# A decoder layer on one core: causal masks of the maxima as 64+64 columns, 25 warm-up transposes, one drain on GpSimd

## The reference

```python
x = layernorm(x + attn(x))          # causal self-attention, 16 heads of 16 channels, with biases
x = layernorm(x + xattn(x, ctx))    # cross-attention to 64 context rows, mask on the query side
x = layernorm(x + ffn(x))           # ternary weights, activations rounded to 8 bits, silu(gate) * up

att = einsum('bhqd,bhkd->bhqk', q, k) * 0.25
att = where(tril, att, -inf)        # the causal mask
y   = einsum('bhqk,bhkd->bhqd', softmax(att), v)
```

## Time and profile before

| | |
|---|---|
| time, median of 3 runs | 889.46 us (888.61 to 890.96) |
| profiled execution | 889.83 us, its span 888.1 us |
| TensorE busy | 818.7 us (92%) |
| VectorE busy | 676.0 us (76%) |
| ScalarE busy | 581.7 us (65%) |
| GpSimd busy | 388.2 us (44%) |
| L961, scores of the maxima | 119.0 us in 768 matmuls |
| L965, mask of 128 columns | 53.5 us in 512 matmuls |
| L968, mask of 64 columns | 48.4 us in 512 matmuls |

### The profile page before, as it was taken

One profiled execution on the slowest core, in us unless ns is written; L12 is line 12 of the kernel. 1 busy time (PEld: TensorE's weight loads), 2 busy tenths in 40 slices (PEclk: granted clock), 3 DMA queues, 4 the chain that ended last, 5 costly groups with the idle time before them and its releaser, 6 DMA issues.

```text
span 888.1 us, 21732 instructions
## 1 busy us (share of the span) xinstructions
PE 818.7 (92%) x8199; PEld 383.3 (43%) x8225; DVE 676.0 (76%) x1179; ACT 581.7 (65%) x759; POOL 388.2 (44%) x621
## 2 busy tenths in 40 slices
PE   7788889899999999999999999999999999998875
PEld 4433334343554434534454344543535443445533
DVE  6888798558877698877997589774898857835588
ACT  3177765367874588565775669666597469864485
POOL 6533284545343345533434634462524413452244
PEclk9999999999999999999999999999999999999999
DMA  7543123210420111120331112120220000010001
GB/s 207 172 119 82 38 63 94 73 37 19 114 73 2 37 36 39 43 84 2 73 85 49 34 28 49 44 69 16 54 58 25 26 2 1 2 49 1 2 1 49
DMA packets 47814, 45.50 MB, mean 51 GB/s; under 512 B 9698, under 2 KB 43874, under 8 KB 47714
## 3 DMA queue, kind: packets, MB, share of 16 engines
q1 hardware_dynamic: 43698, 39.12, 16.1%
q0 software_dynamic: 1536, 3.15, 1.5%
q10 hardware_dynamic: 2480, 1.84, 0.8%
HBM read 14.55 MB, written 4.19 MB: 21 GB/s over the span
## 4 chain that ended last, share of the span: by engine, by line
PE 77%; DVE 11%; ACT 7%; issue 3%; DMA 1%; POOL 1%; SPq 0%; POOLq 0%; DVEq 0%; ACTq 0%
PE ps L1002 15%; PE ps L987 14%; PE ps L799 10%; PE ps L961 7%; PE ps L814 6%; DVE shift L1316 5%; PE ps L933 4%; PE ps L860 3%; ACT probs L1105 3%; PE ps L945 2%; PE ps L788 2%; DVE shift_h L1316 2%; PE ps L890 2%; PE ps L871 2%; PE ps L885 2%
## 5 line engine op out<-in xcount | busy, mean ns | idle before, releaser
L1105 ACT ACTIVATE probs<-ps 128x1024 f32<-128x1024 f32 (+3 forms) x384 | 297.5, 810 | 148.8 <-PE ps L987 146.0
L1316 DVE TENSOR_REDUCE shift<-ps 128x2 f32<-128x1024 f32 (+2 forms) x224 | 249.8, 1145 | 53.4 <-PE ps L961 28.1
L987 PE MATMUL ps<-q_stack,k_stack 64*128 64x512 bf16 (+3 forms) x1536 | 179.5, 325 | 12.5 <-DVE shift L1316 3.8
L688 POOL TENSOR_SCALAR_AFFINE_SELECT probs<-probs 128x512 f32<-128x512 f32 x128 | 81.1, 639 | 193.2 <-ACT probs L1105 192.6
L1002 PE MATMUL ps<-probs,v_aug 128*32 128x512 f32 (+3 forms) x1536 | 158.8, 497 | 0.7 <-POOL probs L688 0.6
L961 PE MATMUL ps<-k_stack,q_stack 64*128 64x512 bf16 (+3 forms) x768 | 119.0, 327 | 15.6 <-ACT probs L1105 5.6
L1316 DVE TENSOR_REDUCE shift_h<-ps 128x4 bf16<-128x512 f32 (+2 forms) x96 | 98.0, 1046 | 18.6 <-PE ps L968 18.2
L987 PEld LDWEIGHTS ps<-q_stack,k_stack 64*128 64x128 bf16 x1536 | 54.0, 94 | 116.5 <-ACT probs L1105 37.2
L961 PEld LDWEIGHTS ps<-k_stack,q_stack 64*128 64x128 bf16 x768 | 39.7, 93 | 115.5 <-ACT probs L1105 38.9
L1229 DVE TENSOR_REDUCE shift<-ps 128x8 bf16<-128x512 f32 x64 | 40.6, 685 | 26.5 <-PE ps L871 26.4
L1002 PEld LDWEIGHTS ps<-probs,v_aug 128*32 128x32 f32 x1536 | 33.6, 108 | 48.8 <-issue 37.4
(11 more groups left out here) (186 smaller groups left out, 1391.7 us busy)
## 6 DMA issues: line engine op xcount, KB each, us to landing
q_stack<-part_sb SPq DMA_DIRECT2D x168, 64.0 KB, 2.0
k_stack<-part_sb SPq DMA_DIRECT2D x144, 64.0 KB, 2.0
xT<-in_x_cols SPq DMA_DIRECT2D x8, 512.0 KB, 4.9
xt<-in_x SPq DMA_DIRECT2D x8, 512.0 KB, 3.9
out_x<-xt SPq DMA_DIRECT2D x7, 512.0 KB, 3.0
k_stack<-part_sb POOLq DMA_DIRECT2D x48, 64.0 KB, 2.3
q_stack<-shiftT SPq DMA_DIRECT2D x128, 1.0 KB
q_stack<-part_sb ACTq DMA_DIRECT2D x24, 64.0 KB, 2.7
```

The source lines that it names most:

```text
L688: pool.affine_select(out=blk, in_=blk, compare_op=ALU.is_ge, fill=0.0, base=0, pattern=[[0, HG], [1, P]], channel_multiplier=-1).then_inc( ...
L987: mm = pe.matmul(ps[:, u.banks[i], 0:BANK - off], k_stack[rows, part, h, kb * P:(kb + 1) * P], q_stack[rows, part, c, h, off:BANK], start= ...
L1105: act.activation(probs_of(b, n)[:, 2 * p:2 * p + 2, :], pair(u)[:, :, 0:BANK - off], ACT.Exp).then_inc(probs_ready, 1)
L1316: dve.tensor_reduce(to[:, :, pairs[0]:pairs[-1] + 1, qb % TH], pair(u)[:, :, 0:len(pairs) * w].rearrange("p j (h w) -> p j h w", w=w), AX. ...
```

## The change

`pick_h` grows from 192 to 256 columns, and what it and `causal` hold changes: the second half of `causal`'s columns now has the mask of the second 64 keys, and `pick_h[rows, 0:128]` and `pick_h[rows, 128:256]` are the weights for the first and the second 64 keys. For this GpSimd runs six selections per row half instead of two. `max_unit` adds the mask in two parts of 64 columns each. The number of mask matmuls and their place in the order stay. TensorE's transposes at the start go from 15 to 25, and GpSimd executes a drain after `make_masks`.

```diff
--- before.py
+++ after.py
@@ -330,7 +330,7 @@
         ident, ident_h = sb("ident", [P, P]), sb("ident_h", [P, P], BF16)
         ones, ones_h = sb("ones", [P, P]), sb("ones_h", [P, P], BF16)
 
-        pick_h, causal = sb("pick_h", [P, P + HALF], BF16), sb("causal", [P, P], BF16)
+        pick_h, causal = sb("pick_h", [P, 2 * P], BF16), sb("causal", [P, P], BF16)
 
         maskT = sb("maskT", [TK + H, T], BF16)
         off_pick = sb("off_pick", [TK + H, H, TK], BF16)
@@ -621,10 +621,18 @@
             made(pool.memset(pick_h[:], 0.0))
             made(pool.memset(causal[:], 0.0))
             for rows in four:
-                made(pool.affine_select(out=pick_h[rows], in_=pick_h[rows], compare_op=ALU.not_equal, fill=1.0, base=HALF,
-                                        pattern=[[-1, P + HALF]], channel_multiplier=1))
+                made(pool.affine_select(out=pick_h[rows], in_=pick_h[rows], compare_op=ALU.not_equal, fill=1.0, base=0,
+                                        pattern=[[-1, 2 * P]], channel_multiplier=1))
+                made(pool.affine_select(out=pick_h[rows], in_=pick_h[rows], compare_op=ALU.not_equal, fill=1.0, base=P + HALF,
+                                        pattern=[[-1, 2 * P]], channel_multiplier=1))
+                made(pool.affine_select(out=pick_h[rows, P + HALF:2 * P], in_=pick_h[rows, P + HALF:2 * P], compare_op=ALU.not_equal,
+                                        fill=0.0, base=1 - HALF, pattern=[[0, HALF]], channel_multiplier=1))
+                made(pool.affine_select(out=pick_h[rows, P:P + HALF], in_=pick_h[rows, P:P + HALF], compare_op=ALU.not_equal,
+                                        fill=1.0, base=1 - HALF, pattern=[[0, HALF]], channel_multiplier=1))
                 made(pool.affine_select(out=causal[rows], in_=causal[rows], compare_op=ALU.is_ge, fill=NEG, base=0,
-                                        pattern=[[-1, P]], channel_multiplier=1))
+                                        pattern=[[0, 2], [-1, HALF]], channel_multiplier=1))
+                made(pool.affine_select(out=causal[rows, HALF:P], in_=causal[rows, HALF:P], compare_op=ALU.not_equal, fill=NEG,
+                                        base=1 - HALF, pattern=[[0, HALF]], channel_multiplier=1))
             made(pool.memset(shift_h[:], 0.0))
             made(pool.memset(q_stack[:, 1, :, :, :].rearrange("p c h q -> p (c h q)").bitcast(F32), 0.0))
             pool.memset(v2[:], 1.0).then_inc(consts_ready, 1)
@@ -677,6 +685,7 @@
                         move_piece(pool, g, n, first_main, first_rest)
                     if (g, h) == (1, 1):
                         make_masks()
+                        pool.drain()
                 if u.kind == "tern":
                     n = u.idx
                     pool.wait_ge(tern_ready, n + 1)
@@ -806,7 +815,7 @@
                 if kind == "kq":
                     t, e, h = pieces[u.idx]
                     if b == 0 and u.idx == 0:
-                        stir(u, 15)
+                        stir(u, 25)
                     if b == 0 and u.idx < 2:
                         pe.wait_ge(kq_loaded[1 - t], 16)
                     pe.wait_ge(x_loaded[h], 16 * (b + 1))
@@ -961,12 +970,11 @@
                         mm = pe.matmul(ps[:, u.banks[s], end - w:end], q_stack[rows, 0, c, h, qb % TH * P:(qb % TH + 1) * P],
                                        k_stack[rows, 0, h, k0:k0 + w], start=True, stop=not diag)
                     if diag:
-                        for s, rows in enumerate(four):
-                            pe.matmul(ps[:, u.banks[s], end - P:end], pick_h[rows, HALF:P + HALF], causal[rows, :],
-                                      start=False, stop=False)
-                        for s, rows in enumerate(four):
-                            mm = pe.matmul(ps[:, u.banks[s], end - HALF:end], pick_h[rows, 0:P], causal[rows, 0:HALF],
-                                           start=False, stop=True)
+                        for part in range(2):
+                            at, keys = slice(part * P, (part + 1) * P), slice(part * HALF, (part + 1) * HALF)
+                            for s, rows in enumerate(four):
+                                mm = pe.matmul(ps[:, u.banks[s], end - P + part * HALF:end - HALF + part * HALF], pick_h[rows, at],
+                                               causal[rows, keys], start=False, stop=part == 1)
                 mm.then_inc(max_scores, 1)
 
             def scores(u):
```

## The result

| | before | after |
|---|---|---|
| median | 889.55 us (4 runs) | 879.95 us (879.04 to 880.97, 4 runs) |
| ratio | | 0.9891, 95% interval [0.9874, 0.9908] |
| profiled execution | 889.83 us, span 888.1 | 879.04 us, span 877.3 |

The kernel got 9.6 us faster, not 5.4. The time lies under the range of the forecast, and the two parts that the forecast counted (4.5 for the masks, 1.2 for the warm-up) cannot fill the gap. Further on, a time beside a ratio is a median, and the gain or loss beside it is worked out from the ratio where nothing else is said.

What follows compares the result with a forecast made beforehand. TensorE was taken as the bound, with 77% of the chain of waits and 96% busy in the middle. 889.83 - 4.5 (masks) - 1.2 (warm-up) = 884.1 us, mask building and drain 0; 8-in-10 range 881.5 to 888.8.

Steps and rivals of the forecast that it cites:

- Masks, -4.5 us: Diagonal-block mask matmuls on TensorE, first pair 64 wide instead of 128: 4.5 us less, ends 3.0 and 7.7.
- The pitch of 0.03 us for narrow pairs: TensorE's 64-column mask pairs pass in 0.03 us, against 0.06 for wide ones, saving 0.030 us a pair.
- The rule on weight loads: TensorE's mask matmuls: about 81 ns a matmul at 128 columns, set by loads too, so narrowing gives 0.
- Building the masks, 0: GpSimd's longer set-up at the start, 3.6 us covered by idle time: 0, ends 0 and +1.0 us.
- Warm-up, -1.2 us: 25 transposes on TensorE at the start raise the clock earlier: two thirds of 1.76 us, 1.2 us less.
- The rule that transposes do not count for the clock: TensorE's start: transposes do not count as busy for the clock, so the warm-up costs its whole 1.1 us.
- case 3: Start on TensorE: warm-up buys nothing and delays by 1.1 us, masks still gain 4.5; 886.4 us, chance 0.13.
- The drain, 0 with ends 0 and +0.2 us: Added GpSimd drain after the masks are built ends inside a 7 us wait for ScalarE: costs 0 to 0.2 us.
- rival 4: TensorE's clock falls more often as mask work thins, 1.65 us a fall; five falls give 893.6 us, chance 0.09.

Runs made afterwards that it cites:

- the doubled masks: The kernel before with every mask pair of 128 columns given twice: 899.17 us, 1.0101 [1.0083, 1.0119].

## Why the prediction was wrong

- **Masks, -4.5 us: right.** Alone they gave 4.6, with an interval of 3.3 to 5.9. The pitch of 0.03 us for narrow pairs held. The split of it was a little off: I took 4/5 of the 5.6 us on the chain; what holds is 0.6 of all 7.7 us.
- **The rule on weight loads** that the forecast set aside (the Trainium skill, "TensorE: Matmul & The Clock Gate", "Back-to-back issue gap") would have made this part 0; the measured 4.6 us settles it for these pairs of half-height matmuls.
- **Building the masks, 0: right.** GpSimd's constants are ready at 13.0, expected at 13.2. GpSimd's own first move comes 0.7 us late for it (expected 0.3), and the chain to the first maximum does not wait for that move.
- **Warm-up, -1.2 us: right.** -1.2 alone, 1.5 on top of the rest, both small beside their intervals; the traces show it better, where ScalarE's first copy starts 1.55 and 1.66 us earlier than with 15 transposes, 1.2 us earlier than with one. The 25 transposes span 5.16 and 4.73 us, under the 5.8 of the low rate, and the first projection behind them runs at 2.4 GHz; so the engine had run only transposes before the clock rose. The rule that transposes do not count for the clock (the Trainium skill, same page, "Part 4: PE-mode transpose") made case 3; the runs contradict it.
- **The drain, 0 with ends 0 and +0.2 us: this step failed.** It brought 4.5 us alone and 3.3 on top of the other two parts. I priced the added drain where it stands (it is indeed covered, 2.03 us in 7 us of idle time) and never asked what it takes off later work. The kernel has 18 drains of its own, and the trace of before showed the one that mattered: GpSimd idle for 5.83 us "<-issue" before L708, TensorE for 3.53 us "<-issue" before L871, and 2.88 us of "issue" on the chain. I read that the chain had 3% of "issue" and did not look where. In these kernels a drain pays 0.084 us for every software DMA since the last drain; the early one takes over 24 of the 48, so the one on the chain is 2.0 us shorter.
- **The clock, as rival 4: right kind, wrong sign.** I asked whether thinner work would add stretches at 1.2 GHz. The wait of 3.5 us for the drain came with such a stretch in the profiles of the kernel before, of the masks alone, of the warm-up alone, of both together and of the doubled masks, and in no profile with a shorter drain; filling the wait gave 2.0 us back by the ratio, 1.5 at its place in the profiled pair. So 2.0 us are drain and about 1.5 clock, which makes the 3.3 to 3.6 us that the first qcast brings in the profiled pairs. The 1 us or so by which the ratio of the drain alone lies above that is not explained; its interval begins at 3.5 us. Where the other stretches of low clock fall differs from profile to profile, and what steers them stays open. The forecast missed the median by 4.2 us, which the 3.3 to 4.5 of this step cover. The profiled pair is 10.8 us apart, and the differences at 802 us (1.6 us gained) and at 132 us (1.1 us lost), where one of the two has a fall of the clock and the other has not, are tied to no part of the change by any run.

## What to carry to other kernels

Search the trace for idle time "<-issue" on the chain of waits and look up which instruction of the sequencer fills it; here it was a drain. GpSimd's drains cost 0.084 us here for each software DMA (64 KB) since the last one, beside the time that work in flight takes (the 2.8 us of additions). So put one into idle time ahead of the one that is waited for, or give those DMAs to SyncE, and read from the trace of your kernel what they cost there. When a part's own cost is covered, ask in the same breath what it takes away from an instruction of the same kind later.

## What the runs showed that was not expected

- A GpSimd drain after 48 software DMAs took 3.99 us, after 24 of them 2.01 to 2.03 us. How long ago the DMAs were issued made no difference: the last of them was issued 9 us before the added drain (2.03 us), 43 us before the first qcast of the kernel after (2.01), and 135 us before it where SyncE has the other moves (2.03).
- With a wait of 3.4 to 3.6 us on TensorE came 3.4 us at 1.2 GHz, in all five profiles that have it (before: granted clock 0.69 in 165 to 170, 0.97 in 170 to 175); with 1.6 us of wait the clock stayed, in all four.
- Transposes alone raise TensorE's clock: with 25 of them it was at 2.4 GHz for the first projection, in all five profiles that had 25.
- Two drains in idle time, masks and warm-up together have the lowest median here: 877.95 us, 0.9875 of before; the interval overlaps with that of the changed kernel.
